# Routing and mixing of later token groups placed between the expert tiles of earlier ones

## The chip, the cores and the metric

The kernel runs on one core of a Trainium2 chip. The metric is the device time of one execution in microseconds: 404.62 us as the median of three runs (403.09 to 405.36). The profile comes from one more execution, whose span, from the first to the last instruction, is 389.1 us.

## What is computed

The input x has 16 sequences of 256 tokens of 128 numbers, 4096 tokens in all, in float32. Each token is normalized (xn). Two branches work on xn.

```
# recurrence: two scales, 64 columns each, a = r * exp(i*theta)
b = (xn @ W_re + b_re + 1j*(xn @ W_im + b_im)) * (1 - r)
h = real(scan(h_t = a*h_{t-1} + b_t));  s = sigmoid(h @ W_gate + b_gate) * h
# experts: top 2 of 8, weights w = softmax over the two logits
logits = xn @ Wg + bg;  topv, topi = top_k(logits, 2);  w = softmax(topv)
for each slot: xs = xn * w;  y = (silu(xs @ W1[e]) * (xs @ W3[e])) @ W2[e]
g = silu(xn + y_0 + y_1);   out = x + s * g
```

W1 and W3 are 128 x 512 per expert, W2 is 512 x 128.

## The kernel before

Products in float32 accuracy are made of three passes: each operand is split into a high part, written by ScalarE ("hi"), and a low part, the difference, written by VectorE ("lo"). TensorE adds hi*hi, hi*lo and lo*hi.

The program has two blocks with a barrier between them, `dispatch` and `experts`.

`dispatch` goes over four groups of eight tiles of 128 tokens (`NG`, `GT`). For a group q, TensorE transposes xn (`tokens_t`), makes the router's logits, projects (`projection`, two halves), applies the recurrence as a product with a table (`mixing`, for the first and the second 128 tokens of a sequence), transposes h (`h_t`), multiplies by the gate weights (`gate`) and transposes the tanh back (`tanh_back`). The order is written out by hand: while group q is routed on VectorE, TensorE mixes group q - 1. VectorE's routing is a chain of some twenty small instructions: largest logit, its index, the second largest, a mask, a running count (`prefix`), a TensorE product over the partitions (`pos_at`), and from it each row's place in the region of its expert in `rows_dram`. The softmax of two logits is Exp, an addition, a reciprocal and a product. ScalarE scales the rows by their weight, and POOL scatters them, 16 indirect DMAs a group (L343). The expert weights come in eight triples of DMAs into two buffers (`ew_raw`); ScalarE writes their hi parts (L370), VectorE the lo parts (L500), for the first two experts POOL (L331). POOL also makes the inverse deviation with a pow (L307). After the last group the counts of the experts give the plan: for each of J = 71 tiles of 128 rows its first row and its expert's weights. SyncE fills up each expert's last tile with padding rows. Only then does the second block begin.

`experts` runs the 71 tiles in turns of eight (`TURN`), the middle turns in a hardware loop on each engine. At the head of a turn SyncE and TensorE load the turn's plan into registers (`loaded`, L905). In tile j TensorE transposes the row tile of j + 1, makes the two hidden products a and c of tile j (`up`, six matmuls of 512 columns, L1073 to L1075), transposes the hidden tile of j - 1 (L1080) and makes the output product of j - 2 (`down`, L1089 and L1090). ScalarE does Silu (L983) and two hi parts, VectorE the product hid (L1028), two lo parts (L1006, L1011) and the sum y (L1018). a, c and the transposed hidden tile have two PSUM banks each, the row transpose and y one each. POOL scatters y to `y_dram` (L949). The row, its index and y have eight buffers each; a row is fetched when the result of eight tiles before is out.

The tail loads the two results of each token in eight chunks, adds them to xn with TensorE (L1118) and, in every second chunk, the two to each other with POOL first (L960); then come Silu, the product with `gated`, the addition of x (L1050) and the store.

## Time and profile before

| | |
|---|---|
| median of the runs | 404.62 us |
| profiled execution, span | 389.1 us |
| around the span (median less span) | 15.5 us |
| TensorE matmul busy | 309.9 us (80%) |
| VectorE busy | 230.5 us (59%) |
| ScalarE busy | 172.6 us (44%) |
| POOL busy | 159.1 us (41%) |
| mean granted TensorE clock | 0.904 of full speed |

Of the profiled execution only the span is recorded; its own time outside the span is not, so the difference to the median of the runs stands for it. A matmul's time in the profile overlaps with the next one's, so what a matmul costs when TensorE is the bound is the distance of two starts, not its duration. "Idle before" is the time that an engine stood still before an instruction, with what released it. The chain of waits gives 57% of the span to TensorE, 5% to issue and 4% to VectorE.

### The profile page before, as it was taken

The page shows a single profiled execution, that of the slowest core. Times are in us where ns is not written, and L with a number is a line of the kernel's source. Part 1 is how long each engine was busy: PE and PEld are TensorE (multiplying, and loading weights), DVE is VectorE, ACT ScalarE, POOL GpSimd, SP SyncE. Part 2 cuts the span into 40 slices and gives each one's busy share as a digit, 9 for nine tenths or more (in the row PEclk, how much of TensorE's full clock was granted, in tenths as well). Part 3 has the DMA queues.
Part 4 walks back from the last instruction along what each step waited for, and adds up shares of the span by engine and source line. Part 5 has one row for each costly group of instructions (what it writes and reads, how often), then busy time and mean ns, then how long its engine had stood idle before and what let it go on. Part 6 is the DMA issues. An engine that isn't in the chain of part 4 may idle for free.

```text
span 389.1 us, 6491 instructions
## 1 busy us (share of the span) xinstructions
PE 309.9 (80%) x1846; PEld 264.8 (68%) x1847; DVE 230.5 (59%) x566; ACT 172.6 (44%) x353; POOL 159.1 (41%) x163
## 2 busy tenths in 40 slices
PE   0927887598730499898997998989989989898991
PEld 0826887487720388786886887869868788787440
DVE  3697999477520166465565664656646657566067
ACT  1537495477320254354453543545435445453031
POOL 3357878877772023243232432433324333333260
PEclk9975898869895599899899998999989999999898
DMA  7755353331230201212213112122121121310395
GB/s 218 235 163 156 123 178 124 128 106 50 63 95 20 55 15 49 82 41 63 72 46 95 38 49 81 45 59 72 47 88 40 47 88 47 95 30 12 124 361 162
DMA packets 40220, 35.63 MB, mean 92 GB/s; under 512 B 5622, under 2 KB 32378, under 8 KB 40204
## 3 DMA queue, kind: packets, MB, share of 16 engines
q1 hardware_dynamic: 33932, 24.24, 21.0%
q0 software_dynamic: 4320, 8.43, 6.1%
q10 hardware_dynamic: 1952, 2.76, 1.9%
q8 instruction: 8, 0.13, 0.2%
q14 instruction: 8, 0.07, 0.1%
HBM read 22.20 MB, written 13.67 MB: 92 GB/s over the span
## 4 chain that ended last, share of the span: by engine, by line
PE 57%; issue 5%; DVE 4%; DMA 0%; ACT 0%; SPq 0%
PE bank L1089 12%; PE bank L1073 9%; PE bank L1075 9%; PE bank L1074 9%; PE bank L1080 8%; PE bank L1090 5%; PE bank L1060 3%; PE bank L1118 3%; DVE pair L1050 2%; DVE pair L1047 1%; DMA row<-rows_dram 0%; DVE hid_t_lo L1011 0%; ACT pair L995 0%; SPq L905 0%; DVE y L1018 0%
## 5 line engine op out<-in xcount | busy, mean ns | idle before, releaser
L949 POOL DMA_INDIRECT y_dram<-y,row x71 | 69.5, 978 | 174.3 <-DVE y L1018 174.3
L1089 PE MATMUL bank<-ew,hid_t_hi 128*128 x284 | 77.5, 350 | 1.9 <-DVE hid_t_lo L1011 1.9
L343 POOL DMA_INDIRECT rows_dram<-rows,slot_row x64 | 68.0, 1063 | 19.6 <-issue 15.3
L1028 DVE TENSOR_TENSOR hid<-bank,silu_a 128x512 f32<-128x512 f32 x71 | 49.1, 692 | 34.7 <-PE bank L1075 34.1
L1090 PE MATMUL bank<-ew,hid_t_lo 128*128 x284 | 64.1, 226 | 0.0
L1073 PE MATMUL bank<-ew,row_t_hi 128*128 x142 | 63.6, 448 | 0.0
L975 ACT ACTIVATE hid_t_hi<-bank 128x512 fp32r<-128x512 f32 x71 | 42.4, 597 | 42.0 <-PE bank L1080 42.0
L1075 PE MATMUL bank<-ew,row_t_hi 128*128 x142 | 57.9, 408 | 0.0
L1074 PE MATMUL bank<-ew,row_t_lo 128*128 x142 | 57.7, 406 | 0.0
L1018 DVE TENSOR_REDUCE y<-bank 128x128 f32<-128x256 f32 x71 | 30.1, 425 | 45.4 <-PE bank L1090 45.4
L1089 PEld LDWEIGHTS bank<-ew,hid_t_hi 128*128 128x128 f32 x284 | 55.5, 195 | 2.3 <-issue 2.3
L983 ACT ACTIVATE silu_a<-bank 128x512 f32<-128x512 f32 x71 | 42.4, 598 | 32.2 <-PE bank L1075 32.2
L1090 PEld LDWEIGHTS bank<-ew,hid_t_lo 128*128 128x128 f32 x284 | 56.2, 198 | 0.0
L1060 PE MATMUL bank<-ident,row 128*128 128x128 f32 x71 | 21.4, 302 | 35.0 <-DMA row<-rows_dram 18.2
L1011 DVE TENSOR_TENSOR hid_t_lo<-bank,hid_t_hi 128x512 fp32r<-128x512 f32 x71 | 48.3, 681 | 0.3 <-ACT hid_t_hi L975 0.3
L1080 PE MATMUL bank<-ident,hid 128*128 128x128 f32 x284 | 44.4, 280 | 0.0
L1080 PEld LDWEIGHTS bank<-ident,hid 128*128 128x128 f32 x284 | 36.9, 145 | 10.2 <-issue 0.8
L971 ACT ACTIVATE row_t_hi<-bank 128x128 fp32r<-128x128 f32 x71 | 19.7, 277 | 50.9 <-PE bank L1060 50.9
L1006 DVE TENSOR_TENSOR row_t_lo<-bank,row_t_hi 128x128 fp32r<-128x128 f32 x71 | 20.0, 282 | 32.1 <-ACT row_t_hi L971 32.1
L1060 PEld LDWEIGHTS bank<-ident,row 128*128 128x128 f32 x71 | 10.2, 144 | 36.7 <-DMA row<-rows_dram 18.4
L1075 PEld LDWEIGHTS bank<-ew,row_t_hi 128*128 128x128 f32 x142 | 27.7, 195 | 6.5
L1073 PEld LDWEIGHTS bank<-ew,row_t_hi 128*128 128x128 f32 x142 | 28.6, 202 | 3.4 <-issue 0.2
(135 smaller groups left out, 484.8 us busy)
## 6 DMA issues: line engine op xcount, KB each, us to landing
ew_raw<-in_L_ffn_W SPq DMA_DIRECT2D x24, 256.0 KB, 3.5
row<-rows_dram SPq DMA_DIRECT2D x71, 64.5 KB, 1.9
xn_dram<-xn SPq DMA_DIRECT2D x4, 512.0 KB, 2.8
x_all<-in_L_attn_x SPq DMA_DIRECT2D x8, 256.0 KB, 2.9
xn_all<-xn_dram SPq DMA_DIRECT2D x8, 256.0 KB, 3.2
pair<-y_dram SPq DMA_DIRECT2D x4, 512.0 KB, 8.2
pair<-y_dram ACTq DMA_DIRECT2D x4, 512.0 KB, 8.7
out<-pair SPq DMA_DIRECT2D x8, 256.0 KB, 2.2
```

The costliest lines, as they stand in the source:

```text
L343: pool.indirect_dma_start(out=rows_dram[:, :], out_offset=bass.IndirectOffsetOnAxis(ap=slot_row[:, k, at:at + 1], axis=0), in_=rows[:, k, ...
L949: pool.indirect_dma_start(out=y_dram[:, :], out_offset=bass.IndirectOffsetOnAxis(ap=row[:, k, D:ROW].bitcast(U32), axis=0), in_=y[:, k], i ...
L975: act.activation(ht_hi[:, b], ht_bank[b][:], ACT.Copy).then_inc(ht_hi_done, 1)
L1011: dve.tensor_tensor(ht_lo[:, b], ht_bank[b][:], ht_hi[:, b].bitcast(F32), ALU.subtract).then_inc(ht_lo_done, 1)
L1028: dve.tensor_tensor(hid[:, k % 2], c_bank[k % 2][:], silu[:, k % 2], ALU.mult).then_inc(hid_done, 1)
L1060: pe.transpose(xt_bank[:, 0:P], row[:, k, 0:D], ident[:]).then_inc(xt_ready, 1)
L1073: pe.matmul(to, xt_hi[:, b], hi, start=True, stop=False)
L1074: pe.matmul(to, xt_lo[:, b], hi, start=False, stop=False)
L1075: pe.matmul(to, xt_hi[:, b], lo, start=False, stop=True).then_inc(ready, 1)
L1080: t = pe.transpose(ht_bank[b][:, c * P:(c + 1) * P], hid[:, b, c * P:(c + 1) * P], ident[:])
L1089: pe.matmul(y_bank[:, 0:2 * D], hi, w, start=(c == 0), stop=False, skip_group_check=True)
L1090: mm = pe.matmul(y_bank[:, 0:D], lo, w[:, 0:D], start=False, stop=(c == NC - 1), skip_group_check=True)
```

## The change

One block takes the place of two. The work is in four phases. After the rows of groups 0 to g are routed, at least `FULL[g]` tiles of 128 rows are full, whatever the routing. These run while later groups are routed and mixed; the last phase has the rest, with the padded tiles. The phases have 9, 16, 16 and 30 tiles and open at tiles 0, 9, 25 and 41.

```diff
+FULL = [-(-(K * GT * P * (g + 1) - E * (P - 1)) // P) for g in range(NG - 1)]
+PHASE = [b - a for a, b in zip([0] + FULL, FULL + [J])]
+OPENS = [0] + FULL
...
+STEPS = {
+    0: (("turn", 0),), 1: (("gate", 0),), 2: (("back", 0),),
+    3: (("project", 1, 0),), 4: (("project", 1, 2),), 6: (("tokens", 2),), 7: (("logits", 2),),
+    8: (("mix", 1, 0),), 9: (("mix", 1, 1),), 11: (("places", 2), ("turn", 1)),
+    12: (("count", 2),), 13: (("gate", 1),), 14: (("back", 1),),
+    15: (("project", 2, 0),), 16: (("project", 2, 2),), 18: (("mix", 2, 0),), 19: (("mix", 2, 1),),
+    21: (("turn", 2),), 22: (("tokens", 3),), 23: (("gate", 2),), 24: (("logits", 3),),
+    25: (("back", 2),), 27: (("project", 3, 0),), 28: (("places", 3),),
+    29: (("count", 3), ("project", 3, 2)), 32: (("mix", 3, 0),), 33: (("mix", 3, 1),),
+    35: (("turn", 3),), 36: (("gate", 3),), 37: (("back", 3),),
+}
+STATS_AT = {2: 1, 3: 15}
+NORM_AT = {2: 5, 3: 20}
+ROUTE_AT = {2: 8, 3: 25}
+ROWS_AT = {1: 0, 2: 13, 3: 30}
+PLAN_AT = {1: 0, 2: 13, 3: 30}
+ROWS_EACH = 3
```

`STEPS` names what TensorE does after tile j. ScalarE and VectorE do their part of a step at the head of tile j + 1. The routing and the planning of a phase are cut into 20 steps each, and VectorE does four of each in a tile (`small_step`). ScalarE normalizes half a group in a tile from `NORM_AT` on and scales three rows in a tile from `ROWS_AT` on; POOL scatters them. Before tile 0 group 0 is routed, its rows are scattered, its plan is made and its mixing done, group 1 is routed, and the weights of all experts are split:

```diff
+            tokens_t(0)
+            group_logits(0)
+            bias_of_h()
+            projection(0, 0)
+            projection(0, 2)
+            pe.wait_ge(made, 9)
+            places(0)
+            count_rows(0)
+            mixing(0, 0)
+            mixing(0, 1)
+            tokens_t(1)
+            group_logits(1)
+            places(1)
+            count_rows(1)
...
+            pe.wait_ge(u_lo_done, NC)
+            transpose_row(0)
+            pe.wait_ge(w_lo_done, E)
+            columns = []
+            for j in range(J):
+                if j in OPENS:
+                    pe.wait_ge(planned, 2 * (phase_of(j) + 1))
+                if turn_of(j):
+                    columns += loaded(mybir.EngineType.PE, J + j, turn_of(j), (E - 1) * 2 * EW)
+                pe.wait_ge(rt_lo_done, j + 1)
+                up(j, columns[j])
+                if j + 1 < J:
+                    transpose_row(j + 1)
+                if j >= 1:
+                    transpose_hidden(j - 1)
+                if j >= 2:
+                    down(j - 2, columns[j - 2])
+                for s in steps_after(j):
+                    step(*s)
```

VectorE before the first tile, and its loop over the tiles:

```diff
+            tokens_lo(0)
+            weights_lo(0)
+            dve.wait_ge(made, 9)
+            for n in range(ROUTE_STEPS):
+                routing(0, n)
+                if 2 <= n < 2 + GT:
+                    statistics(1, n - 2, n - 1)
+            means(1)
+            variance(1)
+            weights_lo(1)
+            projection_lo(0, 0)
...
+            projection_lo(0, 2)
+            shift_of_mean(1)
+            weights_lo(2)
+            for n in range(PLAN_STEPS):
+                planning_step(0, n)
+            tokens_lo(1)
+            weights_lo(3)
+            for n in range(ROUTE_STEPS):
+                routing(1, n)
+                if n in (3, 10, 14):
+                    weights_lo({3: 4, 10: 5, 14: 6}[n])
+            weights_lo(7)
...
+            for j in range(J + 2):
+                for step in steps_after(j - 1):
+                    after_step(*step)
+                for q, at in STATS_AT.items():
+                    if at <= j < at + 2:
+                        statistics(q, (j - at) * HT4, (j - at + 1) * HT4)
+                    elif j == at + 2:
+                        means(q)
+                        variance(q)
...
+                    dve.tensor_tensor(hid[:, j % 2], c_bank[:], silu[:, j % 2], ALU.mult).then_inc(hid_done, 1)
+                small_step(j, 0)
+                if j + 1 < J:
+                    row_lo(j + 1)
+                small_step(j, 1)
...
+                small_step(j, 2)
...
+                small_step(j, 3)
```

Between the last small steps stand hid_t_lo of tile j - 1 and y of tile j - 2.

The banks: a, c, the transposed hidden tile and y have one bank each, and the row transpose uses the first 128 columns of a's bank, so it waits for the Silu of the tile before it:

```diff
+        a_bank, c_bank, hidt_bank = banks[0:3]
+        y_bank, rt_bank = banks[3][:, 0:2 * D], a_bank[:, 0:P]
...
+            def transpose_row(j):
+                pe.wait_ge(row_in[j % TURN], j // TURN * 16 + 16)
+                if j:
+                    pe.wait_ge(silu_done, j)
```

Of the four other banks two hold mixing, gate and, from group 1 on, the projection; two hold the transposed tokens, logits, places and counts. The softmax of two is made from a tanh, and the ScalarE table is loaded once, for Silu:

```diff
-            act.preload_act_table(ACT.Exp)
+            act.preload_act_table(ACT.Silu)
...
+                act.activation(turn_w[:], gap[:], ACT.Tanh, scale=0.5).then_inc(turn_w_done, 1)
...
+                    chain(dve.tensor_scalar(weight[:, 0], turn_w[:], -0.5, 0.5, ALU.mult, ALU.add))
...
+                    dve.tensor_scalar(weight[:, 1], turn_w[:], 0.5, 0.5, ALU.mult, ALU.add).then_inc(weight_done, 1)
```

Smaller edits: x has one input buffer a group instead of two; the weight buffers, the hidden tiles, y and later the pair sums share one region (`stage`), and the loaded pairs lie over the expert weights; ScalarE normalizes (half of group 0, all of the others); all lo parts of the weights are VectorE's; the pair sums of the tail too; the rows of a group have one buffer. SyncE fetches the rows in straight code, and at the first tile of a phase it waits for the plan and for all scatters of that phase's group (`rows_sent`), before the last phase for the padding rows too. The row buffers and y stay at eight.

## Rows read from the trace of the kernel before

**Rows 1.** Windows of all engines: length, busy and count by engine, PEclk, DMA share, GB/s

```profile
0.00:132.20 132.20, 78.47 (x459) 69.98 (x460) 80.75 (x267) 63.68 (x133) 83.75 (x88) 0.81 0.40 125
...
132.20:361.70 229.50, 212.09 (x1349) 186.88 (x1349) 136.42 (x283) 104.15 (x212) 68.48 (x70) 0.96 0.19 56
...
361.70:389.10 27.40, 19.34 (x40) 7.99 (x40) 13.29 (x16) 4.78 (x8) 6.90 (x5) 0.88 0.67 230
```

**Rows 2.** Timeline, end of first stage: start, duration, instruction [idle before <-releaser]

```profile
118.77 0.96 POOL L343 DMA_INDIRECT rows_dram<-rows,slot_row  x1 [0.30 <-issue]
...
126.84 1.28 ACT L965 ACT_TABLE_LOAD   x1 [15.91 <-PEq L111]
...
129.84 0.47 PE L1060 MATMUL bank<-ident,row 128*128 128x128 f32 x1 [18.20 <-DMA row<-rows_dram]
```

**Rows 3.** Timeline, one expert tile and the start of the next

```profile
244.75 0.48 PE L1073 MATMUL bank<-ew,row_t_hi 128*128 x1
...
245.29 0.40 PE L1075 MATMUL bank<-ew,row_t_hi 128*128 x1
...
245.72 0.60 ACT L983 ACTIVATE silu_a<-bank 128x512 f32<-128x512 f32 x1 [0.42 <-PE bank L1075]
...
246.23 0.60 PE L1080 MATMUL bank<-ident,hid 128*128 128x128 f32 x4
...
247.58 0.48 PE L1073 MATMUL bank<-ew,row_t_hi 128*128 x1
```

**Rows 4.** Timeline, TensorE at a loop turn and at the last turn

```profile
260.95 0.32 PE L1060 MATMUL bank<-ident,row 128*128 128x128 f32 x1 [1.92 <-issue]
...
336.50 0.30 PE L1060 MATMUL bank<-ident,row 128*128 128x128 f32 x1 [1.35 <-issue]
```

**Rows 5.** DMA issues (us to landing), then groups by line: busy, mean ns

```profile
ew_raw<-in_L_ffn_W SPq DMA_DIRECT2D x24, 256.0 KB, 3.5
...
L370 ACT ACTIVATE ew<-ew_raw 128x1536 fp32r<-128x1536 f32 x8 | 11.4, 1472 | 0.0
...
L500 DVE TENSOR_TENSOR ew<-ew_raw,ew 128x1536 fp32r<-128x1536 f32 x6 | 10.5, 1749 | 0.0
...
L307 POOL TENSOR_TENSOR rstd<-var_eps,half_power 128x8 f32<-128x8 f32 x4 | 6.7, 1683 | 9.8 <-DVE var_eps L486 9.8
```

**Rows 6.** Timeline, TensorE: eight transposes, logits, two mixings and their end

```profile
51.45 1.04 PE L759 MATMUL bank<-ident,gated 128*128 128x128 f32 x8
...
54.61 0.25 PE L800 MATMUL bank<-route_hi_lo,xt_hi 128*128 128x16 f32 x1 [1.02 <-DVE xt_lo L555]
...
56.39 0.48 PE L714 MATMUL bank<-h_bias_hi,ident_r 128*128 128x512 f32 x1
...
58.38 0.39 PE L714 MATMUL bank<-h_bias_hi,ident_r 128*128 128x512 f32 x1
...
61.60 0.27 PE L706 MATMUL bank<-u_hi,mix_lo 128*128 128x256 f32 x1
```

**Rows 7.** Groups by line, VectorE in an expert tile

```profile
L1028 DVE TENSOR_TENSOR hid<-bank,silu_a 128x512 f32<-128x512 f32 x71 | 49.1, 692 | 34.7 <-PE bank L1075 34.1 <-ACT silu_a L983 0.6
...
L1011 DVE TENSOR_TENSOR hid_t_lo<-bank,hid_t_hi 128x512 fp32r<-128x512 f32 x71 | 48.3, 681 | 0.3 <-ACT hid_t_hi L975 0.3
...
L1006 DVE TENSOR_TENSOR row_t_lo<-bank,row_t_hi 128x128 fp32r<-128x128 f32 x71 | 20.0, 282 | 32.1 <-ACT row_t_hi L971 32.1
...
L1018 DVE TENSOR_REDUCE y<-bank 128x128 f32<-128x256 f32 x71 | 30.1, 425 | 45.4 <-PE bank L1090 45.4
```

**Rows 8.** Timeline, two routing steps of VectorE; group by line, the statistics

```profile
86.86 0.22 DVE L602 TENSOR_REDUCE best_key<-key 128x8 f32<-128x64 f32 x1
...
87.11 0.23 DVE L606 TENSOR_TENSOR chosen<-key,best_key 128x64 f32<-128x64 f32 x1
...
L470 DVE BATCH_NORM_STATS2 stats<-x_in_sb 128x6 f32<-128x128 f32 x32 | 8.5, 282 | 4.4 <-DMA x_in_sb<-in_L_attn_x 4.4
```

**Rows 9.** Group by line, the tail's addition of x

```profile
L1050 DVE TENSOR_TENSOR pair<-pair,x_all 128x512 f32<-128x512 f32 x8 | 8.4, 1049 | 0.3
```

More of the change, by code:

```diff
@@ L29 @@
 HT4 = GT // 2
+ROWS = K * GT
 ROW = D + 1
@@ L196, in dispatch @@
-        ht_bank, gate_bank = u_bank, (banks[4], banks[6])
-        count_at = xt_bank[0][:, 0:E]
+        NMAX = max(PHASE)
+        plan = sb("plan", [1, 2 * J + E], I32)
+        steps = sb("steps", [1, NMAX], F32)
+        count, avail, tile_end, jump, used, taken, hop = (
+            sb(n, [1, E], F32) for n in ("count", "avail", "tile_end", "jump", "used", "taken", "hop"))
+        base = sb("base", [1, 1], F32)
+        padded, tiles_i = sb("padded", [1, E], I32), sb("tiles_i", [1, E], I32)
@@ new lines, in build @@
+        passed = sb("passed", [1, NMAX, E], F32)
+        plan_f, plan_g = sb("plan_f", [1, 2, NMAX], F32), sb("plan_g", [1, NMAX], F32)
+        row = sb("row", [P, TURN, ROW], F32)
+        rt_hi, rt_lo = sb("row_t_hi", [P, 2, P], F32R), sb("row_t_lo", [P, 2, P], F32R)
+        hidt_hi, hidt_lo = sb("hid_t_hi", [P, 2, HID], F32R), sb("hid_t_lo", [P, 2, HID], F32R)
+        banks = [ctx.enter_context(nc.psum_tensor(f"bank{i}", [P, 512], F32)) for i in range(8)]
+        a_bank, c_bank, hidt_bank = banks[0:3]
@@ new lines, in loaded, with turn_of, all_results_out @@
+        def loaded(eng, first, n, most):
+            return nc.values_load_multi_w_load_instructions(
+                plan[0:1, first:first + n], engines=[eng], min_val=0, max_val=most,
+                skip_runtime_bounds_check_because="the plan is clamped to this range on the chip")[1]
+        def turn_of(j):
+            at = j - OPENS[phase_of(j)]
+            return min(TURN, PHASE[phase_of(j)] - at) if at % TURN == 0 else 0
+        def all_results_out(eng):
+            for k in range(TURN):
+                eng.wait_ge(y_out[k], 16 * ((J - 1 - k) // TURN + 1))
@@ L281, in _ @@
-            sp.wait_ge(filled, 1)
-            sp.wait_ge(made, 5)
-            sp.dma_start(rows_dram[IDLE:IDLE + P, :], pad_row[:]).then_inc(pad_out, 16)
-            sp.wait_ge(planned, 3)
-            starts = nc.values_load_multi_w_load_instructions(
-                plan[0:1, 2 * J:2 * J + E], engines=[mybir.EngineType.SP], min_val=0, max_val=IDLE - P,
-                skip_runtime_bounds_check_because="a count of rows is at most TOK")[1]
-            for start in starts:
-                sp.dma_start(rows_dram[bass.ds(start, P), :], pad_row[:]).then_inc(pad_out, 16)
@@ new lines, in tanh_back, with step @@
+            def tanh_back(q):
+                for half in range(2):
+                    pe.wait_ge(tanh_done, q * 2 + half + 1)
+                    for i in range(HT4):
+                        t = pe.transpose(gate_bank[half][:, i * P:(i + 1) * P],
+                                         tanh_t[:, 2 * q + half, i * P:(i + 1) * P], ident[:])
+                    t.then_inc(tanh_ready, 1)
+            def step(name, q, *part):
+                if name == "tokens":
+                    tokens_t(q)
+                elif name == "logits":
+                    group_logits(q)
+                elif name == "places":
+                    places(q)
+                elif name == "count":
+                    count_rows(q)
+                elif name == "project":
+                    projection(q, *part)
+                elif name == "mix":
+                    mixing(q, *part)
+                elif name == "turn":
+                    h_t(q)
+                elif name == "gate":
+                    gate(q)
+                elif name == "back":
+                    tanh_back(q)
```

1308 lines of the change are left out of this document (634 added, 674 removed).

## The prediction

> **What bounds the kernel now.** I read the page's engine and slice rows first, then the windows by stage. They split the 389.1 us into 132.2 us before the first expert matmul, 229.5 us of expert tiles and 27.4 us of tail [rows 1]. The median of the runs is 404.62, so 15.5 us lie around the profiled span; I hold them fixed. The first stage is bound by chains: TensorE is busy 78 of 132 us, at a clock of 0.81. At its end TensorE has been idle since about 112 us, while POOL sends the last row scatters at 1.26 us each (0.96 and 0.30 of issue) until 119.7, then comes the block change with a table load of 1.28 us [rows 2]. In the tile stage the timeline shows TensorE as the bound: tile starts lie 2.83 us apart (244.75, 247.58) [rows 3], and 71 tiles make 200.9 of the 229.5. Seven turns of eight tiles open with an idle "issue" of about 1.94, the eighth, which is outside the loop, with 1.35 [rows 4], 14.9 in all. The other 13.7 are a drain of about 4 and stretches at the 1.2 GHz level (mean clock 0.96).
>
> **The first tile.** The new first tile needs groups 0 and 1 routed and all eight experts' weights split. No scatter of group 1 is needed. Both splits now end on VectorE. The chain, with before's durations: statistics, mean, pow and transposes put group 0's logits at about 17, by my reading of the timeline's start, whose order hardly changes (half of the normalizations move to ScalarE, the bias products come behind the logits). Routing with its interleaved statistics takes 7 to 8 us and ends near 25, held by ScalarE's turn at the softmax. VectorE then does mean and variance 1.0, split 1 1.75, projections and tables 4.8, and waits for POOL's pow (1.7), queued behind six scatters that end at 33, until 34.8 [rows 5]. Split 2 and 19 planning steps of 0.22 bring it to 41, token and weight splits to 44, logits 1 end at 44.5. Routing 1 then carries splits 4, 5, 6, and 7 follows. A split e+2 can only start after the split of e freed its buffer: a transfer (3.5 us by the DMA row, three of them issued over 1.3, so about 5), ScalarE's 1.47 and VectorE's 1.75 [rows 5]. The pairs 4, 6 and 5, 7 pass at about 47.5 to 49.3, 54.4, 57.6, 62.7. Eight register loads (1.35) later the first tile starts: **64.1**, bounds 59 and 73. That is 68.1 earlier. Group 0's scatters (16 times 1.26 from 25.5, paced by ScalarE) end near 46 and its plan near 41: hidden. What hid the weight splits before (the chains of four groups) is mostly gone here, so each us of them counts.
>
> **The work that moves in.** TensorE work of one group at the full clock, by starts: logits 1.8 (54.61 to 56.39), mixing 2.0 and 3.3 (56.39, 58.38, 61.60 and its 0.12), twelve more products in the second mixing than in the first, 1.35, so half a projection 1.4, and eight transposes 0.9 [rows 6]; the gate is six 512-column matmuls, 1.4 to 1.5 by the 0.23 to 0.27 between those of [rows 3]. With tokens 0.9, turn 0.9, back 0.9, places and count 0.3 and two half projections it is 14.4. Groups 2 and 3 bring 28.8, group 1 (without tokens, logits, places) 11.4, group 0 (turn, gate, back) 3.3: **+43.5**, bounds 40 (some hidden in present stalls) and 50 (part at the lower clock). TensorE is the bound here, so all of it is on the path.
>
> **Single banks.** The row transpose now shares the bank of a, so it waits for the silu of the same tile. In [rows 3] the third matmul of a starts 0.54 after the first, silu 0.43 later and takes 0.60: free at 1.57 plus about 0.06, where TensorE would come by at 1.48 (246.23). Cost 0.15 a tile. Nothing else is late in a plain tile: hid (0.69) starts at 1.68 and ends at 2.37, row_lo at 2.68 against a need at 2.98, hid_t_lo (0.68) and the y reduction (0.42) end at 1.08 of the next tile [rows 7]. **+10.7** over 71 tiles, bounds 0 and 25 (0.35 each, the silu latency shown twice).
>
> **VectorE and ScalarE in the mixed tiles.** VectorE's own work is 2.08 a tile [rows 7], 2.2 with dead time, of 2.98. To that come four small steps of 0.25 in routing or 0.2 in planning tiles [rows 8], statistics (0.28 each [rows 8], 1.13 a tile), means 1.0, and 1.3 for a pair of splits (0.68 each). Against TensorE's 2.98 plus its step: tile 17 is 5.3 against 3.0, tiles 12 and 26 4.5 against 3.0, tile 28 4.4 against 3.2, tile 30 4.3 against 3.0, tiles 1, 3, 15, 16 about 5.4 against 4.3; ScalarE in tile 5 (projection, half the normalization) 4.2 to 4.9. The excesses of all tiles add to 16; neighbours absorb some, since TensorE's 0.15 vanishes there too. I take **+12**, bounds 3 and 35. Waits that TensorE newly meets in order (places for the prefix, tokens for the normalization), with the following tile behind them, are about 1 us each, four of them, inside these bounds. POOL needs 4 times 1.26 in a tile that scatters three rows and a result, 5.0 against 3.8 to 5.5, so it falls behind by up to 8 us, which eight row and y buffers cover. Tile 9 is wanted at about 107, its row lands near 102. The row gate of phases 2 and 3 has over four tiles to spare.
>
> **Loops.** All 71 tiles are straight code. Register loads stay: 63 values after the first turn at 1.35 for 9, 0.15 each, **9.5** instead of 14.9, bounds 6 and 14. The loop turns cost 0.6 more than the turn outside the loop, of which one value is 0.15. The Trainium skill, "Runtime: NRT & Kernel Launch", section Instruction fetch mechanics, says that a taken branch out of the fetched window forces a transfer before execution goes on, and so prefers full unrolling. This trace shows at most 0.45 us for it. If the rule's transfer were the larger part of the 1.94, unrolling would give 10 back, not 5.4.
>
> **Rest.** Slow clock and drain 13.7 to **12**: fewer long gaps, but a cold start remains; bounds 8 and 18. Tail: four pair sums move from POOL to VectorE (4 times 0.69, begun while the loads are still waited for). The eight x additions, 8.4 beside POOL [rows 9], fall to 8 times 0.69, the time of hid of the same size [rows 7]: 2.9 back. **26.9**, bounds 25 and 29. The softmax change itself removes one small operation a group, hidden. POOL's two splits go, and with them its neighbour's delays; that is in the 17 to 25 above.
>
> **Sum.** 64.1 + 200.9 + 43.5 + 10.7 + 12 + 9.5 + 12 + 26.9 = 379.6, which is 9.5 less than 389.1. From 404.6: **395.1**.
>
> **Rivals.**
> A. Free mixing: the engines absorb the small work and weights arrive earlier (first tile 60). Then 12 becomes 1 and 64.1 becomes 60: 364.5, so 380. For it: VectorE and ScalarE are busy 136 and 104 of 229.5 [rows 1]. Against: their order is fixed and banks are single.
> B. VectorE becomes the bound, slower than before. In tiles 0 to 38 each split, statistic and routing step sits between hid, row_lo and hid_t_lo, which TensorE wants in the same tile. About 52 us of such work is added; if 34 instead of 12 is not covered, it is 401.6, so 417. It ends on the slower side once over 21.5 is uncovered. For it: plain tiles leave VectorE only 0.8. Against: TensorE has its own step in 25 of those tiles.
> C. Late weights: transfer, ScalarE and VectorE in turn at 10 us a pair in place of 8, also for experts 2 to 5. First tile at 72: 387.5, so 403.
> D. Tanh and Silu don't share a table. The trace has one load for Exp and Tanh and one for Silu, 1.28 each [rows 2]; Tanh beside Silu isn't shown. Twelve loads add 15.4: 410.5. The Trainium skill, "ScalarE: Activation LUTs", section Table sets, lists Tanh with Exp, with which the single load agrees, and doesn't list Silu's set.
>
> **Chances.** Forecast 0.43 (388 to 402.5), A 0.15, C 0.12, B 0.24, D 0.06. About 0.5% (2 us) is what a measurement can tell. Faster: 0.43 and 0.15, and a little of C: 0.60. Same: most of C and the edges of B: 0.13. Slower: 0.27. Range 380 to 413: it leaves out the better part of A and the worst of B.
>
> **What would show it.** First expert matmul at 64 (late weights: over 70, with TensorE released by the weight splits). Tile starts after tile 40 at 2.98 apart: at 2.83 the silu wait is hidden, over 3.2 a bank wait is longer than priced. Tiles 0 to 38 in 39 times 2.98 plus 43.5 plus 12: 172 with loads 177; over 190 means B, with TensorE waiting for VectorE's row_t_lo or hid. More than one table load means D. The register gaps at 1.2. I am wrong if the first tile starts within 64 and the total is over 403 all the same.

## The result and the profile after

The changed kernel took 417.98 us (median of 4 runs, 416.13 to 419.45), the kernel before 404.76 (4 runs) beside it: ratio 1.042, interval 1.038 to 1.046. I had forecast 395.1, in a range that ended at 413. The change is slower here, and by more than the forecast's worst case.

That isn't the whole result. Later runs fell on six numbered chips. On five of them the kernel before took 390 us, not 405, and on the sixth, number 5, it took 401; the number of the result's chip isn't known. On two of the five the changed kernel ran too, and there the change makes next to no difference. Each chip was met on one occasion only, so the chip and the occasion can't be told apart: "slow chip" (the result's and number 5) and "quick chip" below stand for both.

```
chip(s)                    before     changed kernel      ratio
that of the result         404.76     417.98 (4 runs)     1.042  [1.038, 1.046]
quick, number 12           390.55     388.23 (1 run)
quick, number 11           390.24     388.37 (10 runs)    0.9963 [0.9944, 0.9981]
```

From the page of the result's profile (TensorE's line of slices has 10.4 us a digit; it dips at 83 to 104, 145 to 155, 166 to 186, 238 to 249 and 259 to 269):

```profile
span 414.4 us, 6354 instructions
PE 317.5 (77%) x1849; PEld 258.4 (62%) x1849; DVE 227.7 (55%) x593; ACT 181.1 (44%) x380; POOL 145.1 (35%) x163
PE   0838206845899869778998919599999999999873
```

Its windows by stage: first stage, tiles 0 to 41, tiles 42 to 70 with the drain (the last tiles' work after their own products), tail. The columns are the stretch, its length, each engine's busy time, TensorE's granted clock, the DMA share and GB/s.

```profile
0.00:66.28 66.28, 24.61 (x127) 22.68 (x128) 39.26 (x126) 30.31 (x56) 25.28 (x40) 0.76 0.55 170
66.28:288.08 221.80, 180.62 (x1100) 152.41 (x1100) 115.58 (x325) 102.06 (x227) 87.62 (x91) 0.91 0.16 47
288.08:386.00 97.92, 93.46 (x583) 76.22 (x583) 59.21 (x122) 43.92 (x89) 30.94 (x32) 1.00 0.26 79
386.00:414.40 28.40, 18.77 (x40) 7.10 (x40) 13.60 (x21) 4.78 (x8) 1.27 (x2) 0.97 0.67 222
```

The same kernel on quick chip 12:

```profile
0.00:65.47 65.47, 24.92 (x128) 22.91 (x128) 39.22 (x126) 30.32 (x56) 24.89 (x40) 0.77 0.55 172
65.47:260.19 194.72, 174.20 (x1099) 146.26 (x1100) 114.05 (x325) 102.63 (x227) 88.42 (x91) 0.96 0.19 54
260.19:358.50 98.31, 93.52 (x584) 76.28 (x582) 59.53 (x122) 43.97 (x89) 30.30 (x31) 1.00 0.25 78
358.50:386.50 28.00, 18.77 (x40) 7.11 (x40) 13.21 (x21) 4.78 (x8) 0.98 (x1) 0.94 0.67 225
```

Against [rows 1], the first stage fell from 132.2 to 66.3 (65.5 on chip 12) and the tiles grew from 229.5 to 319.7 (293.0). The difference between the two chips, 27.9 us of span, lies almost wholly in the second row, the mixed tiles: 27.1 us, with the same instructions and nearly the same busy times. The plain tiles 42 to 69, with which nothing is mixed, agree to 0.1.

**Where the 27.9 us are.** I took the start of each tile's row transpose in both traces. Phases in which POOL sends rows are tiles 0 to 5, 13 to 18 and 30 to 35. The right half shows the same for another program (the three repairs below), which fell once on the slow chip 5 and once on the quick chip 2.

```
                          changed kernel               with the repairs
us                    result   quick 12  more      slow 5   quick 2   more
before tile 0          61.0      60.4     0.6       66.4     59.9      6.5
tiles 0 to 6           47.0      41.0     6.0       39.3     36.4      2.9
tiles 7 to 12          29.9      29.9     0.0       30.0     28.4      1.5
tiles 13 to 20         47.3      37.7     9.6       47.2     35.9     11.3
tiles 21 to 29         37.5      37.5     0.0       35.2     35.2      0.0
tiles 30 to 37         51.9      34.9    16.9       44.4     32.6     11.8
tiles 38 to 41         13.6      18.7    -5.1       12.3     21.0     -8.8
tiles 42 to 69         89.1      89.2    -0.1       80.0     80.0      0.0
tile 70 and the tail   37.2      37.2     0.1       35.1     36.9     -1.8
```

Nearly all of the loss is in the row phases and the tiles just behind them; on chip 5, 6.5 us are also in the first stage, where the rows of group 0 are sent. Tiles 21 to 29 and 42 to 69 lose nothing on either. A third trace on a slow chip, that of e8 below on chip 5, has its gaps in the same phases (48.1 us in tiles 13 to 20, 46.5 in 30 to 37), but none in the first stage (60.6 before tile 0). Here is the largest of these gaps on the result's chip, from the trace of all engines (start, length, engine, line, what; in brackets the idle time before and what the trace takes for its end):

```profile
238.36 0.97 ACT L523 ACTIVATE rows<-early,weight 128x128 f32<-128x128 f32 x3
239.49 0.39 PE L1101 MATMUL bank<-ew,row_t_hi 128*128 x1
239.69 0.99 POOL L410 DMA_INDIRECT y_dram<-stage,row  x1 [0.31 <-issue]
240.99 0.96 POOL L402 DMA_INDIRECT rows_dram<-rows,slot_row  x1 [0.30 <-issue]
242.26 0.96 POOL L402 DMA_INDIRECT rows_dram<-rows,slot_row  x1 [0.30 <-issue]
243.52 0.96 POOL L402 DMA_INDIRECT rows_dram<-rows,slot_row  x1 [0.30 <-issue]
244.27 0.42 DVE L909 TENSOR_REDUCE stage<-bank 128x128 f32<-128x256 f32 x1 [5.00 <-remote]
245.49 0.99 POOL L410 DMA_INDIRECT y_dram<-stage,row  x1 [1.01 <-issue]
247.88 0.60 ACT L494 ACTIVATE early<-bank 128x512 f32<-128x512 f32 x1 [8.54 <-remote]
249.00 0.69 DVE L894 TENSOR_TENSOR stage<-bank,stage 128x512 f32<-128x512 f32 x1 [4.16 <-ACT stage L585]
249.11 0.45 PE L1085 MATMUL bank<-ident,row 128*128 128x128 f32 x1 [9.23 <-ACT stage L585]
```

TensorE finished its mixing at 238.48, a and c at 239.88; ScalarE, whose copy needs only the mixing, starts it at 247.88, 8.5 us idle, released by nothing that the trace names ("remote"). VectorE's y reduction waits 5.0 in the same way. POOL meanwhile runs on, scatter after scatter, until 246.48. So the gap doesn't begin with TensorE: ScalarE and VectorE start long after their inputs were written. The records of the semaphores say the same: in the three traces on slow chips some updates stand 1 to 10.4 us behind the end of the instruction that made them, all but a few of them in the row phases and just behind, and in the quick traces of the changed kernel and of the repairs none stands over 1 us behind within the span. On the quick chips the same POOL work goes by without such a gap.

### The profile page after: what moved, and what is told of

Its sections match the earlier page's. It is cut to its first block, busy times and chain, and to the rows that moved or that the text cites. A ratio compares the mean times of both kernels' runs of the same rounds, so it can differ in the third digit from the quotient of the medians.

```text
span 414.4 us, 6354 instructions
## 1 busy us (share of the span) xinstructions
PE 317.5 (77%) x1849; PEld 258.4 (62%) x1849; DVE 227.7 (55%) x593; ACT 181.1 (44%) x380; POOL 145.1 (35%) x163
## 4 chain that ended last, share of the span: by engine, by line
PE 64%; issue 9%; ACT 8%; DVE 8%; another core or an unknown queue 6%; DMA 4%; POOL 1%; SPq 0%; POOLq 0%; DVEq 0%; ACTq 0%
PE bank L1118 9%; PE bank L1099 8%; PE bank L1108 8%; PE bank L1101 7%; PE bank L1100 7%; PE bank L1085 5%; PE bank L1119 3%; PE bank L933 3%; PE bank L934 3%; PE bank L935 3%; DVE ew L638 2%; ACT rows L523 1%; ACT ew L467 1%; PE bank L1148 1%
## 5 line engine op out<-in xcount | busy, mean ns | idle before, releaser
L410 POOL DMA_INDIRECT y_dram<-stage,row x71 | 69.7, 982 | 156.6 <-DVE stage L909 146.0
L402 POOL DMA_INDIRECT rows_dram<-rows,slot_row x64 | 65.9, 1030 | 76.9 <-ACT rows L523 61.7
L894 DVE TENSOR_TENSOR stage<-bank,stage 128x512 f32<-128x512 f32 x71 | 49.1, 691 | 77.6 <-PE bank L1101 63.3
L585 ACT ACTIVATE stage<-bank 128x512 f32<-128x512 f32 x71 | 42.4, 597 | 70.6 <-PE bank L1101 61.7
L1099 PE MATMUL bank<-ew,row_t_hi 128*128 x142 | 61.2, 431 | 9.5 <-issue 4.8
L1101 PE MATMUL bank<-ew,row_t_hi 128*128 x142 | 57.0, 402 | 0.0
L1108 PE MATMUL bank<-ident,stage 128*128 128x128 f32 x284 | 45.6, 285 | 0.6 <-DVE hid_t_lo L901 0.6
L1099 PEld LDWEIGHTS bank<-ew,row_t_hi 128*128 128x128 f32 x142 | 27.7, 195 | 14.2 <-issue 10.6
L909 DVE TENSOR_REDUCE stage<-bank 128x128 f32<-128x256 f32 x71 | 29.4, 414 | 6.8 <-remote 5.0
L1108 PEld LDWEIGHTS bank<-ident,stage 128*128 128x128 f32 x284 | 31.5, 145 | 1.3 <-issue 0.9
L1101 PEld LDWEIGHTS bank<-ew,row_t_hi 128*128 128x128 f32 x142 | 27.4, 193 | 6.4
L1100 PEld LDWEIGHTS bank<-ew,row_t_lo 128*128 128x128 f32 x142 | 27.7, 195 | 3.5
```

The source lines that it names most:

```text
L402: pool.indirect_dma_start(out=rows_dram[:, :], out_offset=bass.IndirectOffsetOnAxis(ap=slot_row[:, q % 2, at:at + 1], axis=0), in_=rows[:, ...
L410: pool.indirect_dma_start(out=y_dram[:, :], out_offset=bass.IndirectOffsetOnAxis(ap=row[:, k, D:ROW].bitcast(U32), axis=0), in_=y[:, j % Y ...
L894: dve.tensor_tensor(hid[:, j % 2], c_bank[:], silu[:, j % 2], ALU.mult).then_inc(hid_done, 1)
L1099: pe.matmul(to, rt_hi[:, j % 2], hi, start=True, stop=False)
L1100: pe.matmul(to, rt_lo[:, j % 2], hi, start=False, stop=False)
L1101: pe.matmul(to, rt_hi[:, j % 2], lo, start=False, stop=True).then_inc(ready, 1)
```

## The experiments

All changes are to the changed kernel unless said otherwise. Ratios are to the kernel before on the same chip; 388.4 is the changed kernel's time on the quick chips.

**The two kernels again.**

> The kernel before once more, for its profile. The profiled execution of it had a span of 389.1 us while its timed runs took 403 to 405 us; the changed kernel's had a span of 414.4 us at a time of 416.1 us, only 1.7 us around it. Theory 1 (the forecast's): some 15 us lie outside the span of before, and a new profile again shows a span near 389 with no late semaphore events in it. Theory 2: the first profiled execution was about 14 us quicker than a usual one, and a new one shows a span of 401 to 403 us, with the 12 to 14 us more in stalls of the mixed stages.

> The changed kernel once more, for its profile. The gaps between tiles that no engine's work explains (before tiles 5, 6, 16, 20, 34 and 37, 4 to 14 us each) stand where POOL sends rows and results back to back. If the scatters cause them, they come back before the same tiles and with about the same lengths; if they belong to that one execution, they lie elsewhere. Span 414 to 418 us.

> The changed kernel, timed in turns with the kernel before, and profiled once more. So far the two kernels had been timed as 404.8 and 418.0 us on one occasion and 390.6 and 388.2 us on another. Theory 1: the chip decides; where the kernel before takes 390 us, the changed one takes 388 (ratio 0.990 to 0.998) and its trace shows tiles 0 to 40 within 0.1 us of the earlier quick one except at the row phases. Theory 2: the changed kernel varies by itself, and shows 400 us or more beside a kernel before of 390. Where the kernel before takes 404, theory 1 expects 416 to 420.

Before: 390.31 us at a span of 388.6, thus 1.7 us around it, with the seven timed runs beside it at 389.5 to 391.6. After: 388.23 (span 386.5), then 388.37 in ten runs (span 386.5). Neither theory of the first text holds. A new profile of before shows 389 again, but there are no 15 us around it: every execution since whose span is listed has 1.7 to 1.8 around it. So the profiled one of [rows 1] took about 391 by this estimate, and was not one like the runs of 404.6. Theory 1 of the third text fits: beside a kernel before of 390 us the gaps don't come back at all. That it is the chip and not the occasion isn't shown.

**The row transpose in a bank of its own (e1 from tile 41 on, e8 in all tiles but five).**

```diff
-        y_bank, rt_bank = banks[3][:, 0:2 * D], a_bank[:, 0:P]
+        def rt_bank(j):
+            return (banks[6] if j >= LATE else a_bank)[:, 0:P]
...
-                if j:
+                if j and j < LATE:
                     pe.wait_ge(silu_done, j)
...
-                    if j and c:
+                    if j and (c or j >= LATE):
                         pe.wait_ge(seen, j)
```

> From tile 41 on the row transpose of the next tile goes to a bank of its own (bank 6, free by then) and doesn't wait for silu. Theory: the period of a plain tile is 3.16 us because the transpose waits 0.26 us for silu and the matmul pipeline starts again after it (0.07 us); without the wait it falls to 2.83 to 2.90 us, over 29 tiles 7.5 to 9.5 us less, and total 408 to 410 us. Rival: the next wait in line (the three terms of a for silu, c for the product, hidden transposes) takes it over and the period stays at 3.10 or more, total 416 to 418 us. The mixed tiles 0 to 40 keep their 215 us either way.

> Only the row transpose in a bank of its own, in the mixed tiles too. Against the run that did it from tile 41 on alone (380.2 us): if TensorE bounds the mixed tiles, another 5 to 10 us less, 370 to 375 us; if the other engines or POOL bound them, within 2 us of 380.

e1: 380.17 us, ratio 0.973 (0.968 to 0.978), 8.1 less than the changed kernel. A plain tile takes 2.86, not 3.16; tiles 42 to 69 give 9.2 (79.97 instead of 89.16), and from tile 70 on it takes 2.0 more (39.1 instead of 37.2). TensorE and the silu of one tile in the changed kernel:

```profile
313.50 0.60 ACT L585 ACTIVATE stage<-bank 128x512 f32<-128x512 f32 x1 [1.02 <-PE bank L1101]
313.76 0.40 PE L1101 MATMUL bank<-ew,row_t_hi 128*128 x1
314.25 0.30 PE L1085 MATMUL bank<-ident,row 128*128 128x128 f32 x1
314.38 0.62 PE L1108 MATMUL bank<-ident,stage 128*128 128x128 f32 x4
317.40 0.30 PE L1085 MATMUL bank<-ident,row 128*128 128x128 f32 x1
```

The same in e1:

```profile
313.81 0.60 ACT L589 ACTIVATE stage<-bank 128x512 f32<-128x512 f32 x1 [1.02 <-PE bank L1105]
314.07 0.39 PE L1105 MATMUL bank<-ew,row_t_hi 128*128 x1
314.30 0.27 PE L1089 MATMUL bank<-ident,row 128*128 128x128 f32 x1
314.41 0.60 PE L1112 MATMUL bank<-ident,stage 128*128 128x128 f32 x4
317.16 0.27 PE L1089 MATMUL bank<-ident,row 128*128 128x128 f32 x1
```

Silu ends at 314.10 and the transpose follows at 314.25; in e1 it follows the last matmul's start by 0.23, before the silu's end at 314.41. The theory holds. e8, in which the transposes of rows 0, 7, 8, 23 and 24 stay in the bank of a, fell on chip 5 (before: 401.11): 394.38, ratio 0.985 (0.976 to 0.994), not comparable with 380. Its trace shows tiles 11, 21 and 31 at 2.91, 2.87 and 2.85 where the changed kernel has 3.17, 3.54 and 3.17, and the step tiles shorter by 0.1 to 0.3: where nothing stalls, TensorE with its wait for the silu bounds the mixed tiles too.

**The inverse deviation ahead of the rows (e2).**

```diff
+            inverse_deviation(1)
             for n in range(ROWS):
                 scatter_row(0, n)
-                if n == 5:
-                    inverse_deviation(1)
...
             for j in range(J + 2):
+                for q, at in STATS_AT.items():
+                    if j == at + 3:
+                        inverse_deviation(q)
                 for q, at in ROWS_AT.items():
```

> POOL's inverse deviation (the pow) of a group is issued ahead of the row scatters of that turn instead of behind them, and in the first stage ahead of the 16 scatters of group 0. Theory: VectorE's shift of the mean waited 9.3 us at 99.8 us and 5.4 us in the first stage for that pow; total 5 to 10 us less, 407 to 412 us, and the 12 us that TensorE waits before 57 us shrinks by 2 to 4. Rival: these waits are covered by another one that ends at the same time (the scatters themselves), and the total stays within 2 us of 417.

381.81 us, ratio 0.977 (0.974 to 0.980): 6.4 to 6.6 less. The wait, in the changed kernel on chip 12:

```profile
89.09 0.96 POOL L402 DMA_INDIRECT rows_dram<-rows,slot_row  x1 [0.30 <-issue]
90.35 0.95 POOL L402 DMA_INDIRECT rows_dram<-rows,slot_row  x1 [0.30 <-issue]
91.33 1.67 POOL L387 TENSOR_TENSOR rstd<-var_eps,half_power 128x8 f32<-128x8 f32 x1
93.03 0.17 DVE L633 SCALAR_TENSOR_TENSOR nmr<-moments,rstd 128x8 f32<-128x8 f32 x1 [9.18 <-POOL rstd L387]
```

VectorE's hid, row_lo and y of tile 4 stand behind that nmr, so all engines stand. In e2 it still waits 5.4 us, for POOL's backlog of the turns before. From transpose 5 to transpose 6 it now takes 9.16 instead of 12.95, from 0 to 1 5.24 instead of 7.78 (TensorE's wait before 57 us fell from 12.2 to 9.7, as expected), from 20 to 21 6.45 instead of 7.48; tile 41 takes 1.0 more.

**The order of the tail (e3).**

```diff
-                if c % 2 == 0:
-                    pair_added(c + 1)
+                if c == 0:
+                    pair_added(1)
                 dve.wait_ge(silu2_done, c + 1)
...
+                if c % 2 == 0 and c + 3 < CHUNKS:
+                    pair_added(c + 3)
```

> Only the order in the tail is changed: VectorE makes the pair sum that TensorE needs for an odd chunk one pair of chunks earlier (behind the product of the chunk before, not behind its addition of x). Theory: TensorE's three waits of 1.0 us for pair sums, and ScalarE's waits of 1.5 us behind them, go; a pair of chunks takes 3.0 instead of 3.87 us, the tail is 2 to 3 us shorter, ratio to the changed kernel 0.992 to 0.995. Rival: VectorE's own work (3 operations of 0.69 us per pair more than half of the time) or the output DMAs set the pace, and nothing is gained (within 0.5 us).

386.83 us (median of four, 383.35 to 389.29). The ratio on record, 0.986 (0.981 to 0.992), leaves out the longest of the four; the two medians alone give 0.991. The runs scatter more than the gain, so the trace must say it. TensorE in the last 14 us of the changed kernel:

```profile
372.49 1.12 PE L1148 MATMUL bank<-stage,ident 128*128 128x512 f32 x2 [1.09 <-DVE stage L915]
376.35 1.12 PE L1148 MATMUL bank<-stage,ident 128*128 128x512 f32 x2 [1.02 <-DVE stage L915]
380.22 1.12 PE L1148 MATMUL bank<-stage,ident 128*128 128x512 f32 x2 [1.02 <-DVE stage L915]
```

And of e3:

```profile
373.17 1.02 PE L1150 MATMUL bank<-stage,ident 128*128 128x512 f32 x2
375.89 1.02 PE L1150 MATMUL bank<-stage,ident 128*128 128x512 f32 x2
378.86 1.13 PE L1150 MATMUL bank<-stage,ident 128*128 128x512 f32 x2
```

The waits are gone and from tile 70's transpose to the end it takes 35.1 instead of 36.8: 1.7 us, a little under the 2 to 3 expected. On chip 5 it is 37.0 without this edit (e8) and 35.1 with it (e7). The span of this one execution is the same 386.5 as that of the changed kernel, since the tiles before took as much more, 1.3 of it in tiles 25 and 26, whose code is the same. VectorE is then busy without a gap, which is the rival's bound, reached after the gain.

**The mixing of groups 1 to 3 left out (e5).** The steps "project", "mix", "turn", "gate" and "back" of groups 1 to 3 are taken out of the step table; the output is then not the one asked for.

> Leaves out the projection, mixing and gate of groups 1 to 3 (the gate of group 0 is used for all); their routing, rows and results stay. The forecast priced the TensorE work moved between the tiles at 43.5 us (and 12 us for what VectorE and ScalarE lose by it), added to the tiles. If these add up, the span falls by 43 to 56 us, to 330 to 343 us where the changed kernel has 386.5. Rival: TensorE isn't alone in setting these tiles; POOL's scatters (1.27 us each, 3 rows and one result per tile, 5.1 us, for 17 tiles) are the bound of the row phases, and the span falls by 25 to 35 us only, to 352 to 362 us, with POOL busy without a gap in these phases.

One run: 378.02 us, span 376.3, so only 10.2 less. TensorE's busy time fell by 30.0 (311.4 to 281.4; the forecast's prices for these steps add to 34): my 43 to 56 counted the tokens, logits and group 0's gate, which stay. But of the 30.0 only a third arrives. Tiles 6 to 19 and 21 to 39 fall from 144.2 to 121.0 together, 23 of the 30; then 13 come back. Two lines tell where, VectorE in its turn 19 and TensorE at tile 41:

```profile
160.80 0.17 DVE L627 SCALAR_TENSOR_TENSOR nmr<-moments,rstd 128x8 f32<-128x8 f32 x1 [12.20 <-POOL rstd L381]
245.25 0.48 PE L1079 MATMUL bank<-ident,row 128*128 128x128 f32 x1 [8.21 <-DMA row<-rows_dram]
```

Tile 20 takes 15.3 instead of 7.5, tiles 40 and 41 take 16.3 instead of 11.6. Neither theory had it: POOL's queue is not the bound of every row tile (tiles 14 to 19 run at 3.2), it is a second chain to which these waits tie the tiles, and what TensorE saves ahead of them is given back there.

**Two rows per tile instead of three (e6).** One line, ROWS_EACH = 2.

> Two row scatters per tile instead of three, so each row phase takes 8 tiles instead of 6 and POOL has 3.8 us of scatters per tile instead of 5.1. Theory (POOL's backlog holds the tiles): the wait of VectorE for POOL's power at tile 5 (9 us) shrinks to under 4, the tiles 13 to 18 fall from 4.4 to about 4.2 us each, total 3 to 7 us less than the changed kernel's. Rival: the rows are on the way to the opening of the next phase, and sending them two tiles later moves the wait to tiles 9, 25 and 41: total 0 to 8 us more. Where the chip is one on which the changed kernel takes 418, the gaps of 4 to 14 us at the row phases go or shrink if scatters back to back cause them.

388.08 us in ten runs, ratio 0.995 (0.992 to 0.997): no change. Both texts were right in part. Tile 5 fell from 12.7 to 9.9, but tiles 8 and 9 rose from 4.9 and 5.1 to 9.9 and 7.3, since the rows of group 1 now arrive late for the phase that opens at tile 9. The 4.4 us that this adds come off again at tiles 20, 40 and 41, which take 1.0, 2.5 and 1.4 less: the last phase opens when it did before, and its wait is that much shorter. The wait of tile 9's row:

```profile
114.16 0.48 PE L1085 MATMUL bank<-ident,row 128*128 128x128 f32 x1 [5.08 <-DMA row<-rows_dram]
```

**Bursts on POOL in the plain stage (e9, e10, e11).**

```diff
+                if j in BURSTS:          # (46, 54, 62), BURST = 10
+                    for n in range(BURST):
+                        at = BURSTS.index(j) * BURST + n
+                        pool.indirect_dma_start(out=scratch[:, :],
+                            out_offset=bass.IndirectOffsetOnAxis(ap=extra_ids[:, at:at + 1], axis=0),
+                            in_=pad_row[:], in_offset=None).then_inc(extra, 16)
```

> The changed kernel, with ten more scatters of 64.5 KB (to a scratch tensor) issued by POOL in a row at tiles 46, 54 and 62, where nothing stalls otherwise: POOL is then busy with scatters back to back for about 13 us, three times. The results it delays have eight buffers, enough for the tiles of that time. Theory (scatters back to back hold up the wake-ups of the other engines, on a chip where the kernel before takes over 400 us): a gap of 4 to 12 us in TensorE's row transposes within six tiles behind each burst, 10 to 35 us in all, with all engines waking together when POOL falls idle. On a chip where the kernel before takes 390 us: no such gap, 0 to 3 us more in all. Rival (the stalls belong to the mixed stage's other work, code or place in the program): the plain tiles keep 3.16 us on either chip.

> The changed kernel, with ten memsets of 128x1024 (about 1 us each) in a row on POOL at the same three places instead of scatters. If POOL's being busy is what holds up the others, gaps as with the scatters; if it is the scatters' own traffic, none, and the plain tiles keep 3.16 us (up to 0.3 us more per tile where VectorE and POOL share something), on either kind of chip.

> The three bursts of ten scatters in the plain stage once more. On a quick chip they cost 2.6 to 3.3 us each, through the row buffer that waits for a result to be sent (5 tiles behind the burst), and little else. On a chip where the kernel before takes over 400 us, theory: on top of that, gaps of 4 to 12 us with all engines waking late while POOL issues, so that the stage from tile 46 to 70 takes 100 us or more (88 on a quick chip). Rival: it takes 86 to 90 us there too, and the stalls are not the scatters' doing.

All fell on quick chips. The scatters cost 8 to 11 us (399.60 as the median of two runs, ratio 1.025 (1.012 to 1.037); 396.57 and 399.18 in two repeats of one run), where I had expected 0 to 3; the memsets, 10.09 us in a row, cost nothing (387.61 in eight runs, ratio 0.995). The gaps come five tiles behind each burst:

```profile
293.92 0.33 PE L1100 MATMUL bank<-ident,row 128*128 128x128 f32 x1 [2.65 <-DMA row<-rows_dram]
```

I had counted eight buffers as eight tiles of cover. But row 52 is loaded into the buffer of tile 44 only when that tile's result is sent, which POOL does at 289.4, behind the burst, and without one does some three tiles after the tile. So the cover is five tiles, and the transfer comes on top. The ten memsets end 2.6 us sooner than the scatters and stay inside it, so the pair doesn't tell a busy POOL from the traffic of its scatters. What the bursts were made for, the late wake-ups, was not seen, since none of these chips shows them.

**The repairs together (e7, and e12 on another chip).** e2, e3 and e8 in one kernel.

> The three repairs together: the row transpose in a bank of its own (bank 6, except in the five tiles around the token transposes, where that bank is taken), the inverse deviation ahead of the row scatters, the pair sums of the tail one pair earlier. Theory (the three costs are separate and add up): 8.7 us for the plain tiles, 6.4 us for the inverse deviation, 1.7 us for the tail, and 0.30 us for each of some 35 mixed tiles as far as TensorE bounds them (4 to 10 us): 362 to 368 us where the kernel before takes 390.4, ratio 0.93 to 0.94. Rival: in the mixed tiles VectorE, ScalarE or POOL's scatters (5.1 us a tile in the row phases) hold the tile, the freed 0.30 us go nowhere, and the opening of the last phase (rows and pads on the queues) takes back part: 370 to 374 us.

> The three repairs together once more, beside a new trace of the kernel before on the same chip. If the chip is one where the kernel before takes 390 us: 362 to 368 us, ratio 0.93 to 0.94 (the sum of what the three gave alone, plus 0.3 us per mixed tile, which the trace of the earlier run showed in all of them but the stalled ones). If it takes over 400: 387 to 392 us as before, ratio 0.97.

On chip 5: 390.43 beside 401.11, ratio 0.972 (0.963 to 0.982). On chip 2: 367.49 beside 390.12, ratio 0.940 (0.937 to 0.944), so 20.9 us below the changed kernel, of which 8.1 + 6.5 + 1.7 are the single gains, and the other 4.6 fit the 0.3 a tile that the bank gives in the mixed tiles. The rival's point is in the trace too: the opening of the last phase, 4.13 us of wait before, is 6.72 now:

```profile
244.78 0.47 PE L1092 MATMUL bank<-ident,row 128*128 128x128 f32 x1 [6.72 <-DMA row<-rows_dram]
```

This version beats both kernels on a quick chip, and the kernel before on chip 5 too (the changed kernel was not run beside it there).

**The kernel before on a slow chip** (three further profiles of it).

> The kernel before, profiled on this chip. If it takes over 400 us here, theory: its 11 to 14 us more than on a quick chip are gaps in the first stage (the scatters of all four groups back to back, POOL 70 to 80% busy from 28 to 100 us), and its tile loop, with one scatter per 2.83 us, has none: first matmul of the experts 10 to 14 us later than at 107 us, loop unchanged. Rival: spread evenly over the loop (a longer period). If it takes 390 us, its trace repeats the earlier ones within 1 us.

390.95, 390.50 and 390.93 us: quick chips each time (3, 2 and 14). There is no trace of it on a slow chip.

## Why the prediction was wrong

**The 15.5 us around the span.** This is the step that failed first: "15.5 us lie around the profiled span; I hold them fixed". No such time was found: 1.7 to 1.8 us lie around every span. On chip 5 the kernel before has a span of 399.3 in its run of 401.11, so it loses some 11 us inside its span that it doesn't lose on a quick chip; on the result's chip it loses 14, and no span of it is recorded there. The changed kernel loses 29.6 on the result's chip (417.98 against 388.4), the repaired one 22.9 on chip 5, both inside the span. By the forecast's own terms the two spans should stand at 389.1 and 379.6; on a quick chip they stand at 388.6 and 386.5, a gain of 2.1 and not of 9.5. So of the 22.9 us by which I was wrong, 15.8 (29.6 less the 13.8 that I had carried along) are what a slow chip adds to the changed kernel beyond what it adds to the one before, and the profile of before did not show it; the other 7.1 (388.4 against 379.6 and 1.7) are in the sum. Its largest error is the term for single banks, 10.7 where it measured some 21; that for the loops is wrong by 8 the other way. The prediction's own sign, a first tile near 64 with a total over 403, is what the result shows.

**First tile.** 64.1 forecast, 65.5 measured (66.3 on the result's chip): right. On the result's chip the split of expert 7 ended at 63.96, where I had 62.7, and the register loads took 2.3 instead of 1.35.

**Work that moves in, VectorE and ScalarE beside it.** Forecast 177 for tiles 0 to 38 with the loads; from tile 1's transpose to tile 40's it is 180.4 on a quick chip. The total is right within 3.4, but by errors that cancel. e8 confirms that TensorE bounds these tiles where nothing stalls. But VectorE waits 9.2 us for POOL's pow in turn 4 and 7.2 in turn 19, and 3.8 and 1.0 of that came back at tiles 5 and 20 when the pow was moved (e2). I had dismissed this: "POOL ... falls behind by up to 8 us, which eight row and y buffers cover". The buffers cover the scatters. They don't cover the deviation that stands in the same queue and that VectorE needs at once (e2: 6.4 us back in all, 2.4 of them before the first tile). The same backlog, and the pads on SP's queue, open the last phase 5.2 us late (tiles 40 and 41), where I wrote "over four tiles to spare". The 293.0 of the tiles less 200.9, 43.5, 21.3 for the banks (71 times 0.30) and 1.5 for the loads leave 25.8; less the 4.8 and the 5.2 it is some 16, where I had 24 for VectorE's and ScalarE's excess, slow clock and drain.

**Single banks.** Priced at 0.15 a tile, measured 0.30 (3.16 against 2.86 in e1). The transpose starts 0.49 after the last matmul of c instead of 0.23: it follows silu's end by 0.15, where I had 0.06, and after the break the next two groups start 0.05 later still (0.13 and 0.38 instead of 0.11 and 0.35). The upper bound of the term held it. The period is 3.16 instead of my 2.98: 5.4 us over tiles 41 to 70. What failed here is the size of the wait, not the mechanism.

**Loops.** The register loads were priced at 9.5; the tiles with such loads at 41, 49, 57 and 65 of the result's trace are 0.10, 0.21, 0.08 and 0.34 longer than their neighbours, so all of them cost 1 to 2 us. That gave some 8 us back and hid part of the errors above. In e1, where the transpose doesn't wait for the silu, these tiles take 2.85 to 2.86 like all others. The heads of before cost 1.94 [rows 4], and nearly all of that is gone: about 13 us, where I had 5.4. Four of its eight heads cost more, for behind them TensorE's granted clock fell to the 1.2 GHz level for a stretch, and the next tile took 4.3 to 4.5 us instead of 2.9. The windows of before show the tile behind the second head, at a mean clock of 0.65, and the one behind the third, at 1.00:

```profile
183.15:187.49 4.34, 4.34 (x19) 3.85 (x20) 0.98 (x2) 1.47 (x3) 0.34 (x1) 0.65 0.53 162
209.70:212.63 2.93, 2.93 (x19) 2.61 (x20) 0.98 (x2) 1.47 (x3) 0.27 (x1) 1.00 0.65 215
```

So some 6 us of the slow clock of [rows 1] belonged to the heads too, and the changed kernel's clock is 1.00 from tile 42 to the drain. The Trainium skill, "Runtime: NRT & Kernel Launch", section Instruction fetch mechanics, prefers full unrolling because a taken branch out of the fetched window waits for a transfer; that the gaps went when the branches did agrees, that a transfer was what they waited for no run here shows. The branch isn't the whole of it: the head outside the loop had cost 1.35 as well [rows 4], and why such loads cost 0.1 to 0.34 now stays open.

**Tail.** 26.9 forecast, 28.0 measured, before 27.4 [rows 1]. The forecast's own terms give 24.5 (27.4 less 2.9) to 27.3 (with all four pair sums), so 26.9 was a choice between them. The additions fell to 0.69 as priced. What I missed is that the pair sums, once on VectorE, stand behind the additions in its order and hold TensorE three times by 1.0 (e3).

**The rivals.** D is refuted: one table load, of 1.28 us. C too: the first tile came at 65.5. A too: the engines did not absorb the small work. B gave the right size (417) by luck, with another mechanism: it wanted the tiles over 190 with VectorE as the bound. They are 212.7 on the result's chip, but there all engines wait, VectorE as long as the rest, and on a quick chip they are 180.4.

**Open.** What delays the wake-ups. For POOL's scatters speak the places (the stretches in which rows are sent, in three programs, on two occasions) and that POOL runs from 230.6 to 246.5 nearly without a break before the gap of 238 to 249 ends. Against: the durations of the scatters are the same on both kinds of chip, and the burst was not seen on a slow one. So it is argued, not shown. One rival is untested: the recording of the execution itself. The three traces on slow chips hold 4,697, 4,761 and 4,818 semaphore updates (e7 and e8 the last two), those of the changed kernel and of the repairs on quick chips 6,237 to 6,250. A quarter is missing. Of the 1,553 that the result's trace lacks beside chip 12's, 950 are in the first stage and in the tiles 0 to 6, 13 to 20 and 30 to 37, but 320 are in tiles 42 to 69, where no time is lost. Whether the losses make the gaps, or both have one cause, no run tells. Where the kernel before loses its 11 to 14 us there is open too.

## What to carry to other kernels

Before a difference between the times and the profiled span is called overhead, check that the profiled execution took as long as the timed ones: what doesn't show in the trace can't be held fixed. When an engine is said to fall behind and buffers to cover it, list every instruction in that queue, also the small one that someone waits for, and count the cover from the buffer's release, not from the number of buffers. When two tasks share a bank, add the hand-over between the engines to the durations, here 0.15 us from the end of the silu to the transpose, and what follows late behind it.

## What the runs showed of the hardware that I had not expected

- The kernel before takes 390 to 391 us on five chips, 401 on chip 5 and 405 on the result's. The changed kernel takes 388.4 and 418.0, with the engines' busy times in the mixed tiles nearly alike (POOL 88.4 and 87.6 us; TensorE 174.2 and 180.6, at clocks of 0.96 and 0.91).
- In the three traces on slow chips a quarter of the semaphore updates has no record, and some are late by up to 10.4 us in the row phases; in the quick traces of the changed kernel and of the repairs none is late by over 1 us.
- Back to back, POOL's scatters come at 1.27 us each (0.96 and 0.30) in the row phases on both kinds of chip; in the first stage single ones took up to 2.60 (chip 12) and 3.08 (e7, chip 5).
- In straight code of 71 tiles the register loads of a turn of eight cost 0.1 to 0.34 us, and nothing to be seen in e1.
